# Keys turned in 32 by 32 blocks by VectorE and moved by transfers, normalisations split over VectorE and ScalarE, and new written-out orders, in a two-layer kernel on one core

## The reference

```python
h = _layernorm(x) * (1 + ca) + sa        # four such normalisations outside, two more inside layer 0
# layer 1, for each of the 8 chunks, W and bb carried from chunk to chunk
Z1 = xk_c @ W + bb                       # needs the keys with the head dimension on partitions
mu = Z1.mean(-1, keepdims=True)
std = jnp.sqrt(Z1.var(-1, keepdims=True) + EPS)
x_hat = (Z1 - mu) / std
y = g * x_hat + be
grad_output = y - (xv_c - xk_c)
gxh = grad_output * g
grad_x = (HD * gxh - gxh.sum(-1) - x_hat * (gxh * x_hat).sum(-1)) / (HD * std)
dW = jnp.einsum('bhkc,bhkd->bhcd', eta * xk_c, grad_x)   # needs the keys with tokens on partitions
Wn, bn = (W - dW, bb - db)
Zq = xq_c @ Wn + bn
out = xq_c + g * ((Zq - mu2) / std2) + be
```

## Time and profile before

| | |
|---|---|
| median of 3 runs | 1000.54 us (998.31 to 1001.5) |
| profiled execution, its own time | 1000.42 us |
| profiled execution, span of the trace | 1002.3 us |
| busy PE | 934.4 us, 93% |
| busy PEld | 712.3 us, 71% |
| busy DVE | 793.2 us, 79% |
| busy ACT | 655.1 us, 65% |
| busy POOL | 352.8 us, 35% |

### The profile page before, as it was taken

The page is one execution under the profiler, slowest core; times in us unless marked ns, Lnnn a source line. Parts: engine busy times, 40 slices in busy tenths (PEclk is TensorE's granted clock), DMA queues, the critical chain, the costliest instruction groups (busy, mean ns, idle before and its releaser), DMA issues.

```text
span 1002.3 us, 27532 instructions
## 1 busy us (share of the span) xinstructions
PE 934.4 (93%) x11158; PEld 712.3 (71%) x11158; DVE 793.2 (79%) x1945; ACT 655.1 (65%) x1246; POOL 352.8 (35%) x460
## 2 busy tenths in 40 slices
PE   7689899999999999999999999999999998899995
PEld 5466466677777776677778786687878775677773
DVE  4955448998979779897889878998878967988963
ACT  2542246698766585689766486699675576686772
POOL 1992002243343231143351332233351433444640
PEclk9789999999999998999999999999999999999998
DMA  9000010000000010000000010000000000000000
GB/s 330 9 2 1 1 43 2 2 2 2 3 1 2 12 43 1 2 2 3 2 12 2 12 44 1 1 3 3 2 13 2 12 22 2 2 2 12 3 2 21
DMA packets 15833, 15.98 MB, mean 16 GB/s; under 512 B 2013, under 2 KB 14301, under 8 KB 15325
## 3 DMA queue, kind: packets, MB, share of 16 engines
q1 hardware_dynamic: 15709, 14.23, 4.7%
HBM read 10.04 MB, written 2.10 MB: 12 GB/s over the span
## 4 chain that ended last, share of the span: by engine, by line
PE 63%; DVE 24%; ACT 6%; issue 4%; POOL 3%; DMA 0%; ACTq 0%; DVEq 0%; POOLq 0%; SPq 0%
PE ps L533 8%; PE ps L592 5%; PE ps L616 4%; PE ps L526 4%; PE ps L598 3%; PE ps L575 3%; PE ps L586 3%; PE ps L515 3%; PE ps L506 3%; PE ps L482 3%; PE ps L473 3%; POOL gbase L1318 2%; PE ps L508 2%; DVE tmp L1111 2%; DVE qmax L994 2%
## 5 line engine op out<-in xcount | busy, mean ns | idle before, releaser
L1318 POOL TENSOR_TENSOR gbase<-zhat,gamma 128x512 f32<-128x512 f32 x64 | 81.2, 1269 | 362.2 <-DVE scl L1105 355.7
L1326 POOL TENSOR_TENSOR zq_sqq<-zq_sqq,qinv 128x512 f32<-128x512 f32 x64 | 69.3, 1085 | 206.0 <-DVE qinv L1128 206.0
L775 ACT COPY w_sb<-ps 65x1024 f32<-65x1024 f32 x66 | 66.5, 1007 | 29.2 <-PE ps L592 28.4
L592 PEld LDWEIGHTS ps<-grad,k_sc 64*65 64x65 f32 x2048 | 69.2, 139 | 21.9 <-issue 18.6
L592 PE MATMUL ps<-grad,k_sc 64*65 64x64 f32 x2048 | 76.3, 225 | 3.5 <-DVE grad L1122 3.4
L533 PEld LDWEIGHTS ps<-w_sb,keys 65*64 65x64 f32 x2048 | 65.4, 138 | 19.1 <-issue 13.2
L533 PE MATMUL ps<-w_sb,keys 65*64 65x64 f32 x2048 | 72.9, 224 | 4.8 <-ACT keys L783 2.4
L533 PEld LDWEIGHTS ps<-w_sb,queries 65*64 65x64 f32 x2048 | 65.1, 138 | 13.0 <-issue 8.6
L533 PE MATMUL ps<-w_sb,queries 65*64 65x64 f32 x2048 | 72.1, 224 | 1.9 <-issue 1.5
L1108 DVE TENSOR_TENSOR gbase<-gbase,ps 128x512 f32<-128x512 f32 x64 | 43.5, 679 | 36.2 <-POOL gbase L1318 31.3
L598 PE MATMUL ps<-h,pack_ttt 128*128 128x128 f32 x512 | 69.8, 279 | 0.5 <-ACT zq_sqq L824 0.2
(11 more groups left out here) (248 smaller groups left out, 2365.5 us busy)
## 6 DMA issues: line engine op xcount, KB each, us to landing
x<-in_x SPq DMA_DIRECT2D x8, 256.0 KB, 3.2
xc<-x SPq DMA_DIRECT2D x16, 128.0 KB, 2.4
out_x<-xc SPq DMA_DIRECT2D x16, 128.0 KB, 2.5
pack_ttt<-in_ttt SPq DMA_DIRECT2D x1, 1216.0 KB
keys<-in_gam_bet_rows SPq DMA_DIRECT2D x1, 1024.0 KB
w_sb<-in_compose SPq DMA_DIRECT2D x1, 1024.0 KB, 9.3
zq_sqq<-in_wmod SPq DMA_DIRECT2D x1, 768.0 KB, 4.6
pack_attn<-in_attn SPq DMA_DIRECT2D x1, 640.0 KB, 8.3
```

What stands on the lines that cost most here:

```text
L592: last = mm(bank[2 * f + c][0:C, h * HD:(h + 1) * HD], k_sc[64 * c:64 * c + 64, HH * f + h, :], grad[64 * c:64 * c + 64, h, :], start=Fals ...
L775: nc.scalar.copy(w_sb[:, f, :, :, :].rearrange("p b h d -> p (b h d)"), ps[0:C, 2 * f:2 * f + 2, :].rearrange("p a c -> p (a c)")).then_in ...
L1318: P.tensor_tensor(gbase[:, cols], zhat[:, cols], gamma2[:, cols], ALU.mult).then_inc(S["g_hat"], 1)
L1326: P.tensor_tensor(heads(zq_hat[:, cols]), heads(zq_hat[:, cols]), per_head(qinv[:, hs]), ALU.mult).then_inc(S["zq_ready"], 1)
```

## The change

The turn `l` leaves PE and ACT. DVE turns `k_tok` in 32 x 32 blocks into a new buffer `k_blocks` (two instructions of 128 x 256), and SyncE moves the blocks to their partitions in `kT1` with eight transfers a slot, each 32 partitions x 8 heads x 32 elements. `a` then waits for the transfers. ACT's copy into `k_tok` waits for the turn of slot g - 2 too. `norm_apply` keeps the reciprocal and gets a small product `off` on DVE; the four large instructions go to ACT (`normalised`, letters `2` and `3`), but for the first pair's ln1. The first state is set from one float32 product in place of three bfloat16 ones, and GpSimd's constants lose the parts for it (24 instructions). SyncE gets an order of its own (`x` move, `l` keys, `t` store). The orders of all engines and the banks are written anew; there are as many slots, steps and fills as before but for the 64 key turns. `WARM` is as it was, but the two fills `kT_17` and `kT_33` that it names are gone.

```diff
             def transposed_hat(name, p, u, sem):
                 b = begin(f"{name}{u}_{p}")
-                pe.wait_ge(S[f"{sem}_{u}"], p + 1)
+                if p or sem != "ln1_hat":
+                    pe.wait_ge(S[f"{sem}_{u}"], p + (sem != "ln1_hat"))
+                else:
+                    pe.wait_ge(S[f"first_hat_{u}"], 1)
...
-                    for part in range(3):
-                        last = mm(bank[n][0:C, :], ident_bf[0:C, 0:C],
-                                  w_parts[:, part, HH * f:HH * (f + 1), :].rearrange("c h d -> c (h d)"),
-                                  start=(part == 0), stop=(part == 2), skip_group_check=True)
+                    last = mm(bank[n][0:C, :], ident[0:C, 0:C], w_first[:, f, :, :].rearrange("c h d -> c (h d)"),
+                              start=True, stop=True, skip_group_check=True)
...
-                elif what == "l":
-                    turned(f"kT_{g}", k_tok[:, cols], lambda: ready(f"k1_{g}"))
                 elif what == "a":
                     b = begin(f"z_{g}")
                     pe.wait_ge(S["w_ready"], (SLOTS + 2) * p + s + 1)
-                    ready(f"kT_{g}")
+                    pe.wait_ge(k_moved[f], K_MOVES * (g // 2 + 1))
                     predict(b, kT1, f)
...
+            def normalised(p, n, u):
+                l, name = L[u], f"ln{(1, 2, 4, 5)[n]}"
+                if p == 0 and n == 0:
+                    return
+                src = l["y"] if n == 1 else x[:, u]
+                act.wait_ge(S[f"{name}_inv_{u}"], p + (n > 0))
+                for t in range(T):
+                    last = nc.scalar.activation(l["hat"][:, t, :], src[:, t, :], ACT.Identity, bias=l["off"][:, t:t + 1], scale=l["inv"][:, t:t + 1])
+                last.then_inc(S[f"{name}_hat_{u}"], 1)
...
                     if g >= 2:
                         act.wait_ge(S["k_scaled"], g - 1)
+                        act.wait_ge(k_turned, g - 1)
                     nc.scalar.copy(k_tok[:, cols], src).then_inc(drained(f"k1_{g}"), 1)
-                elif what == "l":
-                    split_heads(f"kT_{g}", kT1, f)
...
                         act.wait_ge(S["dw_done"], SLOTS * p - 1 + step)
+                        filled(act, f"zq_{SLOTS * p - 2 + step}")
                         state0(step)
...
                 link(V.reciprocal(l["inv"][:, :], l["std"][:, :]))
+                if p or name != "ln1":
+                    V.scalar_tensor_tensor(l["off"][:, :], l["mv"][:, :, 0], -1.0, l["inv"][:, :], ALU.mult, ALU.mult)\
+                     .then_inc(S[f"{name}_inv_{u}"], 1)
+                    return
                 for t in range(T):
                     last = V.tensor_scalar(l["hat"][:, t, :], src[:, t, :], l["mv"][:, t, 0:1], l["inv"][:, t:t + 1],
                                            ALU.subtract, ALU.mult)
...
+                if what == "l":
+                    ready(dve, f"k1_{g}")
+                    if g >= 2:
+                        dve.wait_ge(k_moved[f], K_MOVES * (g // 2))
+                    for half in range(2):
+                        last = V.transpose(k_blocks[:, f, half, :, :], k_tok[:, cols].rearrange("p (h j d) -> p j h d", h=HH, j=2)[:, half])
+                    last.then_inc(k_turned, 1)
...
+            def move_keys(p, s):
+
+                p, s, j, f, g, hs, cols = slot_of(p, s)
+                sp.wait_ge(k_turned, g + 1)
+                if g >= 2:
+                    sp.wait_ge(S["z_squared"], g - 1)
+                elif g == 0:
+                    sp.wait_ge(pool_set, N_POOL_SET)
+                for i in range(4):
+                    for half in range(2):
+                        sp.dma_start(kT1_t[32 * half:32 * half + 32, hs, 32 * i:32 * i + 32],
+                                     k_blocks[32 * i:32 * i + 32, f, half, :, :]).then_inc(k_moved[f], 16)
```

The ends of the orders, where layer 1 of the last pair runs:

```diff
-DVE "...rmmazbaczbcazebcayzeybcazeybcamzeabczyebcamyzebcyazebcayzembaczybcazebcayzeybaczemybcaemyzebcayezybcemmyeymmmmmm"
+DVE "...yllmmazbalczmbcalzebmlcayzeyblaczebcalzyebclmayzebclazeyblcayzebclayzemmblcayzebylcazebylaczebcylazemblcayzeybecamyzbceymeymmmmmmm"
+SP  "xllllllllllllllllxllllllllllllllllttxllllllllllllltltllxlllllltlllllllllltlltt"
```

More of the change, by code:

```diff
@@ L137, in turns @@
     assert all(n in (0, PAIRS * PER_TOKEN[what]) for what, n in taken.items()), taken
-PER_BATCH = [f"ln{n}_{what}" for n in range(1, 6) for what in ("var", "std", "hat")]
-PER_BATCH += ["k_max_ready", "k_stab_ready", "k_shifted", "k_exp", "q_exp", "x_layer0"]
+PER_BATCH = [f"ln{n}_{what}" for n in range(1, 6) for what in ("var", "std", "inv", "hat")]
+PER_BATCH += ["first_hat", "k_max_ready", "k_stab_ready", "k_shifted", "k_exp", "q_exp", "x_layer0"]
 PER_PAIR = [
@@ L233, in build @@
         k_tok = sb("k_tok", [128, HW])
+        k_blocks = sb("k_blocks", [128, 2, 2, HH, 32])
         k_sc = sb("k_sc", [128, H, C])
@@ L280, in build @@
         x_loaded = [new_sem(f"x_loaded_{u}") for u in range(2)]
+        k_turned = new_sem("k_turned")
+        k_moved = [new_sem(f"k_moved_{f}") for f in range(2)]
         out_stored = new_sem("out_stored")
@@ L863, in _ @@
                     layer0(p, step, int(what))
+                elif what in "23":
+                    normalised(p, step, int(what) - 2)
                 elif what == "r":
@@ L929, in norm_apply @@
                                            ALU.subtract, ALU.mult)
-                last.then_inc(S[f"{name}_hat_{u}"], 1)
+                last.then_inc(S[f"first_hat_{u}"], 1)
             def add_row(name, p, u, row):
@@ L976, in layer0 @@
                 elif step == LN1:
-                    filled(dve, f"h3T{u}_{p - 1}")
                     norm_apply("ln1", p, u, x[:, u, :, :])
@@ L1097, in slot @@
                 p, s, j, f, g, hs, cols = slot_of(p, s)
-                if what == "a":
+                if what == "l":
[5 more added lines that the diff above has]
+                    last.then_inc(k_turned, 1)
+                elif what == "a":
                     dve.wait_ge(S["z_squared"], g + 1)
@@ L1183, in _ @@
                     mixing(p, step)
-                elif what in "azbcey":
+                elif what in "lazbcey":
                     slot(what, p, step)
@@ L1221, in _ @@
                     load(name)
-            for p in range(PAIRS):
-                move_x(p)
-                if p + 1 < PAIRS:
-                    load_x(p + 1)
-                for half in range(2):
-                    if p:
-                        store(p - 1, half)
-            for half in range(2):
-                store(PAIRS - 1, half)
+            for what, p, step in turns("SP"):
+                if what == "l":
+                    move_keys(p, step)
+                elif what == "x":
+                    move_x(p)
+                    if p + 1 < PAIRS:
+                        load_x(p + 1)
+                elif what == "t":
+                    store(p, step)
             sp.wait_ge(out_stored, 64 * PAIRS)
@@ L1294, in _ @@
             heads4 = [slice(4 * n, 4 * n + 4) for n in range(4)]
-            then_all(tt(s_w0[:, n, :], s_w0[:, n, :], s_mean[:, n].unsqueeze(2).broadcast_to([C, 4, HD]), ALU.subtract) for n in heads4)
-            then_all(P.tensor_copy(w_first[:, n // 2, 4 * (n % 2):4 * (n % 2) + 4, :], s_w0[:, heads4[n], :]) for n in range(4))
-            for part in range(3):
-                then_all(P.tensor_copy(w_parts[:, part, n, :], s_w0[:, n, :]) for n in heads4)
-                if part < 2:
-                    then_all(tt(s_w0[:, n, :], s_w0[:, n, :], w_parts[:, part, n, :], ALU.subtract) for n in heads4)
+            then_all(tt(w_first[:, n // 2, 4 * (n % 2):4 * (n % 2) + 4, :], s_w0[:, heads4[n], :],
+                        s_mean[:, heads4[n]].unsqueeze(2).broadcast_to([C, 4, HD]), ALU.subtract) for n in range(4))
             loaded(pool, "compose")
```

69 lines of the change are left out of this document (34 added, 35 removed).

## The result

| | before | after |
|---|---|---|
| median, us (range) | 1000.34 (998.31 to 1001.5) | 1040.25 (1033.8 to 1048.83) |
| ratio, 95% interval | | 1.0395 [1.0345, 1.0445] |
| profiled span, us, and granted clock | 1002.3, 0.973 | 1047.0, 0.938 |

The change costs 40 us. The forecast was 988 us, and its range ended at 1006. All times are of fast runs; one of the four runs with the normalisations back on VectorE (1045.5 us) was slow and is left out of its median.

The account below looks back on a forecast made before the run. PE was taken to bound 130 to 820 us, and DVE the last pair alone. Terms -23.5 - 1.0 + 0 + 6.4 + 1.5 + 4.0 = -12.6 us gave 988 us; forecast's own range 980 to 996, whole range 968 to 1006.

Parts of the forecast that it names:

- In this stage PE time is wall time: From 130 to 820 us, layer 1 beside the next pair's layer 0: PE, 97% busy, sets the time.
- the term of -23.5 us: Key turns leaving PE in 130 to 820 us: 48 slots x 0.49 us saved, bounds 22 and 30.
- That it still hides there behind PE: Turns on DVE, 0.8 us a slot, in 130 to 820 us: DVE at 90% hides behind PE, cost 0.
- if DVE stood in the way half the time: Fallback for the turns on DVE in 130 to 820 us: 48 x 0.8 / 2 = 19 us.
- The case on the other side: Rival, chance 0.20: a turn instruction on DVE takes 0.71 us, 1.42 a slot, in all stages; +4 us, 1004.
- ACT was never the bound ... gets lighter: 0: ACT loses 74 us of copies, gains 36 us of normalisations, busy 487 of 690 us in the middle: cost 0.
- +1.5 for the latency: Normalisation through DVE, ACT, PE where the first pair's layer 0 runs alone: +1.5 us, bounds 0 and 4.
- Hidden: 0: Key transfers, last landing 6.8 us after first issue, hide off the recurrence, with 2.5 us slack in the last pair: 0.
- +4 for the transfers' starts: First slot of each pair has no slot ahead to hide 5 us of transfers: 4 us counted, bounds 0 and 16.
- late keys: Rival, chance 0.18: transfers take 1.16 us each; the buffer loop decides from 9.3 us to the last landing; 998 us.
- more is gained: Rival, chance 0.20: last pair absorbs its turns and starts are filled, 977 us; with some PE idle closed, 973.
- the marks set for the profile after: DVE turns 0.40 us, PE busy some 35 us less, both-layer stage 23 us shorter, last pair's slots 8.8 us.

Follow-up runs that it names:

- the square: Four kernels in the new orders, constant keys, no transfers: no turn or turn on VectorE, normalisations on VectorE (1011.3, 1026.0 us) or ScalarE (1030.0, 1026.2).
- the dose: Kernel before, old orders, no key turn on PE, constant keys, plus two 128 x 256 turns a slot on VectorE that nobody reads: 1034.93 us, ratio 1.0336.

## Why the prediction was wrong

The change, put together in five steps from the medians: the turns off PE and the one-product state in the old orders -3.1 us (1000.3 to 997.2); the new orders +14.1 (1011.3); turns on VectorE and normalisations on ScalarE, two parts at once, +14.9 (1026.2); the traffic of the transfers +3.6 (1029.8); the wait for the keys +10.5 (1040.3). Each step is uncertain by 4 to 7 us, the steps depend on their sequence, as the square shows, and all but the two ends are kernels with constant keys.

- **The step that failed first: "In this stage PE time is wall time", and the term of -23.5 us.** Measured: -2.3, with the intervals between 0 and -7. A PE that was busy 97% at a clock of 0.99 and a chain that went from one PE line to the next were read as proof that PE alone sets the pace. What the runs showed in its place: more PE work is time (19.9 us of 31), less is hardly any, because other limits, and perhaps the clock, stand close behind. PE's busy time is not all need, either: where 23.5 us of turns were taken out, it fell by 13.4. A page of the Trainium skill bears on this reading: "Perfetto Trace Analysis", section Identifying the Most-Contended Engine, holds matmul busy time to be a poor measure of how close a kernel is to the engine's peak and points to the weight loads' busy share and the share of peak arithmetic. The weight loads were busy 517.84 of 690 us, 75%, well under the 97% of the products; which of the two is nearer to the engine's peak no run here shows. Nor had PE a quarter of its time to spare: its turns done twice cost 19.9 us.
- **"That it still hides there behind PE": cost 0.** In the old orders the same work, put on the recurrence, costs 37.7 us; in the new orders, with the normalisations still on VectorE, it costs 14.6, and its three middle stages are 18.4 us longer. The prediction's own fallback, 19 us "if DVE stood in the way half the time", was near that. The case on the other side had the right side and the wrong cause: it asked for turns of 0.71 us and gave 1004, and with turns of 0.42 it came to 1040. No row stood behind the 93% at which VectorE "could still feed PE": with the dose the middle was 28 us longer at 87%.
- **"ACT was never the bound ... gets lighter: 0", and +1.5 for the latency.** Counted as engine time that is true, since ScalarE's busy time fell. But PE waits for the normalisation, 7.8 us in all in the kernel after (for ScalarE's L783) where it was 2.3 before (for VectorE's L928); it went from 359 to 484 ns four times over, and a hand-over was added. By itself, in the new orders and without a turn, it costs 18.7 us, where the prediction had only the first pair's layer 0 in mind and 1.5 us.
- **"Hidden: 0" and +4 for the transfers' starts.** The prices held: issues of 0.62 us (0.61 measured), a landing of 2.4 (2.0), 6.8 us in all (7.0 in the median slot). So did the term for the starts, 4.7 us of PE's waits against 4. "Hidden: 0" did not: 6.0 us of waits lie in other slots, and the wait for the keys is worth 10.5 us in all. The mark set for the rival "late keys", PE waiting over 10 us in all, was just met at 10.7, though not by its mechanism, as 7.0 us (8.3 at most) is under the 9.3 from which the loop was to decide, and a second `k_tok` changed nothing. On the disputed price the two pages have the packets of the whole program, their MB and their share of 16 engines' span, before and after:

```profile
q1 hardware_dynamic: 15709, 14.23, 4.7%
...
q1 hardware_dynamic: 154973, 31.04, 15.1%
```

That is 139264 packets more, 17 for each of 16 engines and 512 transfers as the prediction had it, for (0.151 x 1047.0 - 0.047 x 1002.3) x 16 = 1776 us of packet time: 13 ns a packet, where the rival had 68 and the 512 B packets of rows 9 took 34. The traffic as a whole is worth 3.6 us, within the intervals. The Trainium skill's page "DMA: Bandwidth & Descriptors", section "Why small descriptors are slow (HBM only)", confines the penalty to HBM; these rows agree in that no packet of 128 B was dearer than one of 512 B, and its table's rule of 512 B, weighed in the prediction, did not decide here. By the byte the small ones were slower, an estimated 10 B/ns against 15.
- **The new orders had no term at all.** They were mentioned as a possible gain under "more is gained". They cost 14.1 us by the run without turn and with normalisations in place, nearly all of it in the last pair (196.0 us against 182.3).
- **Right:** the turn's price (418 ns against 0.40 us), SyncE's price, GpSimd's preparation and the first state at 0, and the last pair as the place with the least cover (4.4 of PE's 10.7 us of waits for keys fall in its 16 slots, 6.3 in the other 48). Of the marks set for the profile after only the turn's price came: PE's busy time was to fall by 35 us and rose by 12, and the stage with both layers was to be 23 us shorter and is 17 longer.

Left open: which letters of the new orders cost the 14 us (the start of the last pair is the place of some 9 of them, by the trace), what the change would do in the old orders with its transfers, and whether PE's relief would be time if the clock stayed up. None of these was tried. No version measured here is faster than the kernel before beyond what can be told, except those that leave work out.

## What to carry to other kernels

Ask of a busy engine not only what its share is but what comes next when it is relieved: here a second engine stood at 85% and the recurrence close behind, a relief of 31 us gave 2, and 54 us put on the second engine cost 15 or 38, by the place in its order. Price both sides of a swap separately, with a dose: do the work twice where it is, and do it for nobody where it shall go, at the very place in the order where it shall stand. Undo parts in pairs as well as singly, since two edits can hide each other's cost.

## What the runs showed of the hardware

The mean granted clock could be raised, 0.938 to 0.959 over four runs to 0.955 to 0.968, by filling gaps, and the median stayed (1040.25 and 1041.88). A blockwise turn of 128 x 256 float32 on VectorE took 403 to 418 ns from a strided source and 439 from a contiguous one. An activation with a scale and a bias for each partition took 484 ns at 128 x 128 from SBUF, where a copy of that size from PSUM took 266. SyncE issued transfers in a row at 0.61 us each; in 26 of 64 rows of eight one issue took longer than 0.8, up to 1.95. A packet of 128 B from SBUF to SBUF took 13 ns.
